# Low-rank experts inside the rounds of the second cross-attention, item by item

## What is computed

```python
q = (x @ Wq).reshape(B, Tq, 8, 128) * SCALE          # second cross-attention
k = (context @ Wk).reshape(B, Tk, 8, 128) * SCALE
v = (context @ Wv).reshape(B, Tk, 8, 128)
attn = softmax(einsum('bqhc,bkhc->bhqk', q, k))
x = layernorm(x + einsum('bhqk,bkhc->bqhc', attn, v).reshape(B, Tq, 1024) @ Wo + bo)

result = einsum('bsd,od->bso', x, base_w) + base_b    # low-rank experts: base, router, 8 experts of rank 8
gating = softmax(einsum('bsd,ed->bse', x, router_w) + router_b).astype(bfloat16)
mid = einsum('bsd,dr->bsr', x, lora_A)
lora_out = einsum('bsr,erd,bse->bsd', mid, lora_B, gating.astype(float32))
x = layernorm(x + result + lora_out * 2.0)            # the output
```

## Time and profile before

| | us |
|---|---|
| median of three runs | 1117.83 |
| the profiled execution | 1118.2 |
| its span, from the first to the last instruction | 1116.4 |
| rounds of the second cross-attention | about 820 to 1065 |
| block of the low-rank experts | 1065.4 to 1116.4 |

### The profile page before, as it was taken

The page is one execution under the profiler, slowest core; times in us unless marked ns, Lnnn a source line. Parts: engine busy times, 40 slices in busy tenths (PEclk is TensorE's granted clock), DMA queues, the critical chain, the costliest instruction groups (busy, mean ns, idle before and its releaser), DMA issues. The chain is left out here.

```text
span 1116.4 us, 17912 instructions
## 1 busy us (share of the span) xinstructions
PE 1018.3 (91%) x6672; PEld 784.8 (70%) x6672; DVE 579.7 (52%) x1271; ACT 404.0 (36%) x1029; POOL 151.0 (14%) x151
## 2 busy tenths in 40 slices
PE   6899799999999999779999978787899999999884
PEld 4578677787787776579999964455767777776642
DVE  1786545555555555565556553575244444444315
ACT  2556434333333334254444513466233222322100
POOL 0334311011011000023333412100100000000000
PEclk9999899999999999979999998899899999999955
DMA  4500000000000000092111003300000000010001
GB/s 143 183 2 1 29 14 11 6 14 15 0 0 0 0 0 0 1 312 66 50 38 38 1 1 66 67 2 1 28 1 21 9 14 14 15 27 1 1 0 33
DMA packets 24159, 34.21 MB, mean 31 GB/s; under 512 B 3153, under 2 KB 19762, under 8 KB 24098
## 3 DMA queue, kind: packets, MB, share of 16 engines
q1 hardware_dynamic: 24098, 33.39, 10.0%
HBM read 30.63 MB, written 2.75 MB: 30 GB/s over the span
## 5 line engine op out<-in xcount | busy, mean ns | idle before, releaser
L1028 ACT ACTIVATE x_prob<-bank,x_negmax 112x375 f32<-112x375 f32 x128 | 72.2, 569 | 154.0 <-DVE x_negmax L944 154.0
L1661 DVE TENSOR_TENSOR moe_h_low<-moe_sq,moe_h_high 128x448 fp32r<-128x448 f32 x64 | 54.7, 872 | 52.8 <-ACT moe_h_high L1726 39.6
L1702 POOL TENSOR_TENSOR moe_sq<-moe_r 128x448 f32<-128x448 f32 x64 | 64.0, 1002 | 123.2 <-ACT moe_r L1734 104.7
L86 PE MATMUL bank<-moe_w_low,moe_h_high 128*112 128x256 f32 x256 | 71.8, 280 | 0.0
L86 PE MATMUL bank<-moe_w_high,moe_h_high 128*112 128x256 f32 x256 | 71.7, 280 | 0.0
L86 PE MATMUL bank<-moe_w_high,moe_h_low 128*112 128x256 f32 x256 | 71.7, 280 | 0.0
L944 DVE TENSOR_REDUCE x_negmax<-bank 112x1 f32<-112x375 f32 x128 | 64.1, 542 | 8.0 <-PE bank L836 6.0
L1734 ACT ACTIVATE moe_r<-bank 128x448 f32<-128x448 f32 x64 | 34.9, 545 | 86.9 <-PE bank L86 85.3
L1427 ACT ACTIVATE x_prob<-bank,x_negmax 112x375 f32<-112x375 f32 x64 | 36.1, 568 | 72.6 <-DVE x_negmax L1342 72.6
L949 DVE COPY x_prob_t<-bank 125x336 f32<-125x336 f32 x128 | 58.9, 498 | 6.1 <-PE bank L845 4.2
L857 PEld LDWEIGHTS bank<-x_prob_t,x_v 125*64 125x64 f32 x768 | 37.7, 137 | 34.2 <-issue 30.2
(11 more groups left out here) (365 smaller groups left out, 2290.3 us busy)
## 6 DMA issues: line engine op xcount, KB each, us to landing
moe_w<-in_L_ffn_W SPq DMA_DIRECT2D x16, 512.0 KB, 4.7
ctx_t<-in_ctx_t SPq DMA_DIRECT2D x8, 376.0 KB, 4.3
x_ctx_t<-in_ctx_t SPq DMA_DIRECT2D x8, 376.0 KB, 3.1
wk<-in_L_xattn_Wk SPq DMA_DIRECT2D x2, 1024.0 KB, 6.7
wv<-in_L_xattn_Wv SPq DMA_DIRECT2D x2, 1024.0 KB, 9.5
wq<-in_L_xattn_Wq SPq DMA_DIRECT2D x2, 1024.0 KB, 11.5
wo<-in_L_xattn_Wo SPq DMA_DIRECT2D x2, 1024.0 KB, 13.1
w_in<-in_L_attn_W_in SPq DMA_DIRECT2D x1, 1160.0 KB, 7.1
```

Source lines behind the costliest of these rows:

```text
L86: last = pe.matmul(out, lhs, rhs, start=(k == 0), stop=(k == len(pairs) - 1))
L1028: act.activation(PROB(u, e)[:, :], S_BANK(u, e)[0:T, 0:S], ACT.Exp, bias=negmax[:, g:g + 1], accum_out=total[:, g:g + 1]).then_inc(p_ready, 1)
L1661: dve.tensor_tensor(h_low[half][:, m, :], sq[m % 2][:, :], h_high[half][:, m, :].bitcast(F32), ALU.subtract).then_inc(low_done, 1)
L1702: pool.tensor_tensor(sq[m % 2][:, :], r[m % 2][:, :], r[m % 2][:, :], ALU.mult).then_inc(sq_done, 1)
```

## The change

The block `low_rank_experts` is gone. Its work is done in the rounds of `wide_cross_attention`, which has one further round on TensorE (`for i in range(B + 2)`). Three kinds of job are new, and they go through the same bank `JOB`. A third place in a step, `MID`, lies between `turn` and `weigh`.

- `BASE` of item i-2 stands late in `u` = 3: two products of 272 columns with `xt`. The third one, of the bias row, is gone: VectorE adds the bias (loaded for all 112 rows) instead, its 256 columns in place of the copy in `normalize`, its 16 others in `base`. VectorE empties `BASE` in `base`, at the end of `u` = 3: it adds router and mid columns with bias, adds the base part to `x`, takes the negative maximum and doubles mid.
- ScalarE takes the exponentials of the gates with their sum (`gate_exps`) and VectorE makes the gated product (`gates`), both at `u` = 0 of the next round.
- `GATES` of item i-3 stands mid in `u` = 1: one transpose, emptied by ScalarE.
- `LOW` of item i-3 stands mid in `u` = 2: one product with `lora_b`, emptied by VectorE in `add_low`, which also takes the statistics; ScalarE makes the deviation (`end_deviation`) in `u` = 2, VectorE normalises (`finish`) in `u` = 3, and SyncE stores the item.
- Items 6 and 7 are finished behind the loop. The weights of the experts are loaded ahead of the third context.

```diff
-        if u == 3 and late and i == B:
-            return [(NT, i - 1)]
+        if u == 1 and at == MID and i > 2:
+            return [(GATES, i - 3)]
+        if u == 2 and at == MID and i > 2:
+            return [(LOW, i - 3)]
+        if u == 3 and at == LATE and i > 1:
+            return [(BASE, i - 2)] + ([(NT, i - 1), (BASE, i - 1)] if i == B else [])
...
+        if i > B:
+            return {(1, MID): [(GATES, B - 2), (GATES, B - 1)], (2, MID): [(LOW, B - 2), (LOW, B - 1)]}.get((u, at), [])
...
             def _(sp):
                 for i in range(B):
+                    if i == 2:
+                        core.load_lora_weights(sp, d)
...
-                core.load_lora_weights(sp, d)
+                for i in range(B):
+                    sp.wait_ge(out_ready, i + 1)
+                    sp.dma_start(output[i], core.x[:, i, :]).then_inc(stored, 16)
+                sp.wait_ge(stored, 16 * B)
...
+                    elif kind == BASE:
+                        last = accumulate(pe, out[0:T, 0:W], [(core.xt[:, c, i * T:(i + 1) * T], w_base[:, c, :]) for c in range(KD)])
+                    elif kind == GATES:
+                        last = pe.transpose(out[0:E1 * RK, 0:T], gm[:, i, :, :].rearrange("t e r -> t (e r)"), ident[0:T, 0:T])
+                    elif kind == LOW:
+                        last = pe.matmul(out[0:T, 0:D], gm_t[:, i, :], lora_b[:, :], start=True, stop=True)
...
                         if i < B:
                             turn(i, u)
-                        if u == 0 and i > 0:
+                        for job_ in jobs(i, u, MID):
+                            job(job_)
+                        if u == 0 and 0 < i <= B:
                             weigh(i - 1, 1)
...
-                    chain.link(dve.tensor_copy(core.x[:, i, :], normed[:, :]))
+                    chain.link(dve.tensor_tensor(core.x[:, i, :], normed[:, :], base_bias[:, 0:D], ALU.add))
+
+                def base(i):
+                    n = number[(BASE, i)]
+                    dve.wait_ge(job_ready, n + 1)
+                    dve.tensor_tensor(small[:, i, :], JOB[0:T, D:W], base_bias[:, D:W], ALU.add).then_inc(small_ready, 1)
+                    dve.tensor_tensor(core.x[:, i, :], JOB[0:T, 0:D], core.x[:, i, :], ALU.add).then_inc(job_used, 1)
+                    dve.wait_ge(small_ready, i + 1)
+                    dve.tensor_reduce(top[:, i:i + 1], small[:, i, 0:E1], AX_X, ALU.max, negate=True).then_inc(top_ready, 1)
+                    dve.tensor_scalar(mid2[:, i, :], small[:, i, E1:E1 + RK], 2.0, None, ALU.mult)
+
+                def add_low(i):
+                    n = number[(LOW, i)]
+                    dve.wait_ge(job_ready, n + 1)
+                    dve.tensor_tensor(core.x[:, i, :], JOB[0:T, 0:D], core.x[:, i, :], ALU.add).then_inc(job_used, 1)
+                    dve.wait_ge(job_used, n + 1)
+                    dve.bn_stats(end_stats[:, i, :], core.x[:, i, :]).then_inc(end_stats_ready, 1)
...
                         if u == 3 and i > 0:
                             normalize(i - 1)
+                        if u == 2 and i > 2:
+                            add_low(i - 3)
                         if after:
                             normalize_heads(*after)
+                        if u == 0 and i > 2:
+                            gates(i - 3)
+                        if u == 3 and i > 2:
+                            finish(i - 3)
...
+                        if u == 3 and i > 1:
+                            base(i - 2)
+                gates(B - 2)
+                base(B - 1)
+                gates(B - 1)
+                for i in (B - 2, B - 1):
+                    add_low(i)
+                for i in (B - 2, B - 1):
+                    finish(i)
...
                         after = following(i, u)
                         if after:
                             exps(*after)
+                        if u == 0 and i > 2:
+                            gate_exps(i - 3)
...
+                gate_exps(B - 2)
+                gate_exps(B - 1)
+                for i in (B - 2, B - 1):
+                    drain((GATES, i))
+                for i in (B - 2, B - 1):
+                    end_deviation(i)
```

More of the change, by code:

```diff
@@ L1054, in _, with wide_cross_attention @@
                 rounds(act, round_)
-def wide_cross_attention(core, d):
+def wide_cross_attention(core, d, output):
     nc = core.nc
@@ L1067, in wide_cross_attention @@
     QUERY, CTX_MAIN, CTX_REST, OUT, NT = "query", "ctx_main", "ctx_rest", "out", "nt"
+    BASE, GATES, LOW = "base", "gates", "low"
+    EARLY, MID, LATE = range(3)
     TURNS = [("q", c, g) for c in range(KD) for g in range(2)] + [("k", 0, 0), ("k", 0, 1), ("k", 1, 0)]
@@ L1224, in job @@
                         pe.wait_ge(normed_ready, i + 1)
+                    elif kind == BASE and i == 0:
+                        pe.wait_ge(core.lora_loaded, 80)
+                    elif kind == GATES:
+                        pe.wait_ge(gm_ready, i + 1)
                     work(JOB, job_).then_inc(job_ready, 1)
@@ L1281, in _ @@
                     prepare(len(first) + n, job_)
-                for i in range(B + 1):
+                for i in range(B + 2):
                     for u in range(J):
@@ L1287, in _ @@
                             scores(i + 1, 0)
-                        for job_ in jobs(i, u, 0):
+                        for job_ in jobs(i, u, EARLY):
                             job(job_)
@@ L1295, in _ @@
                             weigh(i, 0)
-                        for job_ in jobs(i, u, 1):
+                        for job_ in jobs(i, u, LATE):
                             job(job_)
@@ L1320, in empty @@
                     return copy(cn[i % 2][:, :, 128:DC], src[0:SP_, 0:ST * CB].rearrange("s (k d) -> s k d", k=ST), None)
+                if kind == GATES:
+                    return copy(gm_t[:, i, :], src[0:E1 * RK, 0:T], None)
                 assert kind == NT
@@ new lines, in gates @@
+                def gates(i):
+                    dve.wait_ge(gate_e_ready, i + 1)
+                    dve.reciprocal(gate_inv[:, i:i + 1], gate_sum[:, i:i + 1]).then_inc(gate_inv_ready, 1)
+                    dve.wait_ge(gate_inv_ready, i + 1)
+                    dve.tensor_scalar(gate[:, i, :], e_gate[:, i, :], gate_inv[:, i:i + 1], None, ALU.mult).then_inc(gate_ready, 1)
+                    dve.wait_ge(gate_ready, i + 1)
+                    shape = [T, E1, RK]
+                    dve.tensor_tensor(gm[:, i, :, :], gate[:, i, :].unsqueeze(2).broadcast_to(shape),
+                                      mid2[:, i, :].unsqueeze(1).broadcast_to(shape), ALU.mult).then_inc(gm_ready, 1)
@@ L1458, in _ @@
                     prepared(len(first) + n, job_)
+                on_vector = (OUT, BASE, LOW)
                 for i in range(B + 1):
@@ L1463, in _ @@
                             exps(*after)
-                        for job_ in jobs(i, u, 0):
-                            drain(job_)
+                        if u == 0 and i > 2:
+                            gate_exps(i - 3)
+                        for job_ in jobs(i, u, EARLY) + jobs(i, u, MID):
+                            if job_[0] not in on_vector:
+                                drain(job_)
                         if u == 0 and i > 0:
                             collect(i - 1, 1)
+                        if u == 2 and i > 2:
+                            end_deviation(i - 3)
                         if u == 2 and i < B:
```

149 lines of the change are left out of this document (43 added, 106 removed).

## The result

The changed kernel takes 1098.23 us in the median of four runs (1097.45 to 1099.52), beside 1117.1 for the kernel before (four runs). The ratio is 0.983, with a 95% interval from 0.981 to 0.986. In a second series the medians were 1101.05 (six runs, 1098.30 to 1104.66) and 1117.51 (eleven runs), ratio 0.986 (0.983 to 0.988). The forecast was 1099, and both lie in its range. The profiled execution took 1098.13, its span 1096.3.

The account below looks back on a forecast made before the run. TensorE was taken to bound the rounds, with the experts' block at half clock behind: span 1116.4 - 35.4 (end) + 16.5 (rounds) = 1097.5, with 1.8 around it 1099.3; median 0.4 less, 1099 us. Range 1094 to 1105.5.

Parts of the forecast that it names:

- Rounds: All rounds of the stage together: the added jobs and their waits on one bank lengthen them by 16.5 us.
- `LOW`: Step 2, rounds 3 to 7: a 1.3 us wait plus 0.45 of work, 1.75 each, 8.75 us together.
- `BASE`: Step 3: 1.12 us in each of rounds 2 to 5, 4.5 together; hidden in a gap in rounds 6 and 7.
- `GATES`: Step 1: 0.5 us in each of rounds 3 to 5, 0.75 in round 6, nothing in round 7; 2.25 together.
- the query job: Queued behind `BASE` on the shared bank: it waits 0.35 us in each of three rounds, 1.0 us together.
- The bias add of unknown shape: VectorE's add in `normalize`, both operands from SBUF: between 0.29 and 0.42 us, taken as 0.42.
- The end: Behind the last `weigh`: last projection starts 2.6 us later, but the span ends at 1081.0 instead of 1116.4, gaining 35.4.
- Rival 1: At the end, the clock falls ahead of the last projection: 1101.5 to 1104.7 us, in the middle 1103; chance 0.22.
- Rival 2: The end stays at full clock because there are jobs in it: 1097 us; chance 0.12.
- Rival 3: Bank hand-overs in the rounds cost less, without the wait ahead of `LOW`: 6.5 us less, 1092.5; chance 0.06.
- Rival 4: New gaps in each round let the clock fall mid-round: slower than before, 1127 us; chance 0.04.
- Rival 5: Finishing of items waits until the end, stores in a burst: 5 us more, 1104; chance 0.06, shared with missed small waits.

Follow-up runs that it names:

- e1: The changed kernel with `LOW` of items 0 to 4 written to an idle bank instead of the jobs' bank: 1095.21 us, ratio 0.980.
- e2: The changed kernel with `LOW` moved behind `weigh`, ahead of the output projection, in the same bank: 1095.37 us, ratio 0.980.
- e3: The changed kernel with `GATES` of items 0 to 4 written to a free bank instead of the jobs' bank: 1103.58 us.
- e12b: The changed kernel with two useless ScalarE copies ahead of emptying `NT` in rounds 3 to 7, lengthening the wait ahead of `LOW`: 1110.31 us, ratio 0.992.
- e6e: The changed kernel with useless matmuls filling TensorE's waits behind the last output projection: 1098.8 us.
- e5c: The kernel before, with the one-row bias product dropped, VectorE adding the bias, and the weights loaded earlier: 1101.16 us, ratio 0.986.
- e9c: The changed kernel with free banks for `GATES` and `LOW` of items 0 to 4, and free banks and a new job order at the end: 1083.27 us, ratio 0.970.
- e10b: The kernel before, with the bias product given 128 input rows, each 1/128 of the bias, and the weights loaded earlier: 1105.44 us, ratio 0.989.
- e11b: The changed kernel with the one-row bias product back in `BASE` and no bias add on VectorE: 1103.83 us, ratio 0.987.
- e0: The changed kernel run again with nothing altered, six runs, the second series: 1101.05 us, ratio 0.986.

## Why the prediction was right, and what it missed

**Rounds.** Forecast 16.5 us, measured 19.9 - 2.9 = 17.0. Compared start by start with the kernel before, a middle round grew by 1.92 in step 2 (`LOW`; forecast 1.75), 1.16 by `BASE` (1.12), 0.62 by `GATES` (0.50), 0.13 by the query job (0.35) and 0.08 by the `weigh` behind the wait, 3.91 in all, where the forecast had 3.72. Two errors in `LOW` cancelled, which is luck: its wait was 1.14 and not 1.3, and its work took 0.61 us and not the 0.45 of back-to-back products. What is left of its 1.92 is 0.17, as ahead of the wait the tail of `turn` no longer overlaps with anything. With `GATES` taken at 0.75 in round 6 the stretch from `OUT(4)` to `OUT(5)` came out within 0.15, and with `BASE` hidden in round 6 the next one within 0.3. The bias add of unknown shape took 0.43 us, the upper end of its bounds, as I took it:

```profile
974.24 0.43 DVE L1423 TENSOR_TENSOR x<-x_normed,lora_bias 112x256 f32<-112x256 f32 x1
```

**The end.** The last projection starts 2.9 us later instead of 2.6, and 22.5 us follow its start instead of 22.1. The order of the jobs and the place where the clock falls were those of the forecast. The copy of `GATES`, 0.25, which had no row, takes 0.25.

**Sum.** 1.2 us too much gain in the stage, and 2.4 of scatter ahead of it in the other direction: the forecast of 1099.0 hit 1098.2, but it is right to about 1 us by its steps, and no better.

**Rivals.** Rival 1, the clock falling ahead of the last projection, did not happen in the profile of the change, but it did in e1, e2, e3 and e12b, where the projection took 6.8 to 8.0 us for 5.43: four of the eight profiles with this order of jobs at the end. Its price there, 1.4 to 2.5 us, is at most that of its lower bound (2.5); the projection wholly at half clock, its upper one, was never seen. So it is a matter of the single execution. The spread of 6 us in the second series may come from falls like this one, as it goes with the granted clock, but its slower runs have no trace. Rival 2's price, 2, was confirmed by e6e at 2.2 in the trace. Rival 3 had the right target: the wait it wanted gone was really there, and e1 took it away for 6.05. Rival 4's mechanism exists (e3, e12b), but not its size: I let the clock stay low once fallen, which made 28 us a round; it came back within some 7 us each time, and cost 1.6 to 3.1. Rival 5 did not occur: the items 0 to 4 were stored in the rounds, though the first store was issued only at 991.23, since SyncE's queue takes the last context load (990.82) first.

**What the forecast did not ask.** It took half clock in the block as given, as the price of a place at the end: "Eight items at full clock make 12.4 us, against 33.3 now. That is the gain on TensorE alone". (The two are not quite alike: 12.4 counts the turns of `GATES`, and 33.3 leaves them out; with their 1.70 it is 35.0.) The gain was real, the reading of where it came from was not: 16 of the 33 us go with eight products of a single row (e5c). The rows to see it stood in the prediction's own groups: the clock was back within 10 us at the start of the stage, while TensorE was busy for 15.07 of 16 us at 0.51 in the block. A full engine that stays at half clock did not fit what the start of the stage showed, and I passed over it. Had it been asked, the bias add on VectorE would have been seen as the part that brings most of the gain, and the move of the gates and of the low-rank part as one with a cost of 15.5 and a yield of 13.2.

## What to carry to other kernels

When TensorE is busy without a gap and still at half clock, look at what it is fed before moving work: a product of one input row for a bias costs as much as a full one, and among otherwise full products it can keep a clock down that has already fallen. Work moved into a loop that is bound by TensorE pays for the hand-overs of a shared bank about as much as for itself (3.91 us a round here, and 2.07 with free banks in e9c); give it a bank that is idle just then, and it pays only its own products. And short waits of 1 to 2 us in a busy loop carry a risk beyond their length, since the clock may fall behind them in one execution and not in the next.

## What the runs showed of the hardware

- A matmul of one input row against one of 128, all else equal: the clock stays at 0.50 for 25 us of uninterrupted products, or is back at 1.00 after 5 (kernel before, e10b). Its duration is no shorter than that of full products: at half clock two instructions of 272 columns took 1.24 us with one row (kernel before) and 1.11 with 128 (e10b), at full clock 0.71 with one row (e11b) and 0.62 with 128.
- With TensorE at full clock and two such instructions among the 172 of a round, nothing happens to the clock (e11b, 1.00 in the rounds). What the chip counts, these runs do not tell.
- A wait of 1.14 us in a busy loop left the clock alone in both profiles of the change and in those of e6e and e11b, and brought it down in one round of five of e3; one of 1.95 did so in three of five rounds (e12b).
- The same kernel, run six times on one chip, spread over 6.4 us (e0), and its reordered version with fewer gaps over 1.4 (e9c, five runs).
